# Steps of two head pairs: side jobs between the projections, and their readers moved up on the other engines

## What is computed

```python
h = _layernorm(x) * (1 + ca) + sa
q, k, v = h @ W_q, h @ W_k, h @ W_v
a = sigmoid(h @ W_gate + b_gate)
# per head, over the 256 tokens of a batch
S = a_t[..., None] * S + k_t[..., None] * v_t[..., None, :]
o_t = einsum('bhk,bhkv->bhv', q_t, S)
x = x + ga * (out @ W_o)
h = _layernorm(x) * (1 + cb) + sb
probs = sigmoid(h @ router_w.T + routing_bias); the best TOP_K = 2 of E_ROUTED = 8
x = x + gb * (shared expert(h) + weighted routed experts(h))
```

## Time and profile before

| | us |
|---|---|
| median of 3 runs | 1460.13 |
| lowest, highest | 1457.93, 1462.41 |
| the profiled execution | 1457.31 |
| its span | 1455.2 |
| busy: PE, DVE, POOL, ACT | 1251.1 (86%), 1018.9 (70%), 949.2 (65%), 710.3 (49%) |

### The profile page before, as it was taken

One profiled execution on the slowest core, in us unless ns is written; L12 is line 12 of the kernel. 1 busy time (PEld: TensorE's weight loads), 2 busy tenths in 40 slices (PEclk: granted clock), 3 DMA queues, 4 the chain that ended last, 5 costly groups with the idle time before them and its releaser, 6 DMA issues. The chain is left out here.

```text
span 1455.2 us, 35430 instructions
## 1 busy us (share of the span) xinstructions
PE 1251.1 (86%) x10935; PEld 1086.1 (75%) x10935; DVE 1018.9 (70%) x2183; ACT 710.3 (49%) x1637; POOL 949.2 (65%) x1288
## 2 busy tenths in 40 slices
PE   6999888989888888898989798989797989999970
PEld 5888777777777777776878686868686879889860
DVE  6777767666767676677676666667675647788757
ACT  4665554555454555454545454545454444444420
POOL 4356676758585757676767676766667637777755
PEclk9999999999999999999999999999999999999995
DMA  8900102020111202020202020202021136665336
GB/s 241 262 6 25 60 20 80 23 74 32 65 54 42 83 13 96 2 94 2 94 6 91 7 89 7 89 7 89 17 81 66 49 114 197 192 186 177 100 121 227
DMA packets 88445, 119.30 MB, mean 82 GB/s; under 512 B 9652, under 2 KB 52327, under 8 KB 88384
## 3 DMA queue, kind: packets, MB, share of 16 engines
q1 hardware_dynamic: 79296, 101.47, 22.1%
q0 software_dynamic: 9088, 17.07, 3.4%
HBM read 50.29 MB, written 61.79 MB: 77 GB/s over the span
## 5 line engine op out<-in xcount | busy, mean ns | idle before, releaser
L1188 DVE TENSOR_TENSOR pairs<-qk_banks,pairs 128x512 f32<-128x512 f32 x256 | 164.9, 686 | 131.4 <-PE qk_banks L1536 131.3
L595 POOL TENSOR_SCALAR pairs<-pairs 128x512 f32<-128x512 f32 x128 | 91.8, 717 | 197.7 <-ACT pairs L752 197.4
L1637 PE MATMUL vo_bank<-A,shared 128*64 128x256 f32 (+1 forms) x2048 | 202.6, 342 | 15.4 <-POOL A L510 14.6
L1176 DVE TENSOR_TENSOR_SCAN pairs<-pairs,shared 128x515 f32<-128x515 f32 x128 | 161.7, 1264 | 73.3 <-POOL pairs L593 67.7
L1181 DVE TENSOR_TENSOR_SCAN pairs<-pairs,shared 128x515 f32<-128x515 f32 x128 | 170.4, 1331 | 48.6 <-POOL pairs L595 48.6
L710 POOL DMA_INDIRECT y_dram<-pairs,y_row x156 | 158.0, 1013 | 68.4 <-issue 44.2
L1622 PE MATMUL score_banks<-pairs 64*128 64x128 f32 x2048 | 192.6, 286 | 3.2 <-ACT kx L779 3.2
L1637 PEld LDWEIGHTS vo_bank<-A,shared 128*64 128x64 f32 x2048 | 132.3, 141 | 72.7 <-issue 23.7
L1622 PEld LDWEIGHTS score_banks<-pairs 64*128 64x128 f32 x2048 | 146.6, 188 | 25.6 <-issue 25.6
L1577 PE MATMUL vo_bank<-big,h_hi 128*128 128x512 f32 x128 | 63.4, 495 | 117.9 <-DVE next_row L1160 66.5
L758 ACT ACTIVATE shared<-vo_bank 128x512 f32<-128x512 f32 x128 | 76.4, 597 | 168.9 <-PE vo_bank L1579 168.9
(11 more groups left out here) (252 smaller groups left out, 3241.2 us busy)
## 6 DMA issues: line engine op xcount, KB each, us to landing
rows_dram<-pad_row SPq DMA_DIRECT2D x17, 2112.0 KB, 8.0
ga_all<-rows_dram SPq DMA_DIRECT2D x39, 264.0 KB, 2.8
pairs<-y_dram SPq DMA_DIRECT2D x16, 512.0 KB, 5.0
pairs<-in_L_ffn_gate_w_dram SPq DMA_DIRECT2D x39, 128.0 KB
pairs<-in_L_ffn_up_w_dram SPq DMA_DIRECT2D x39, 128.0 KB
ga_all<-in_L_ffn_down_w_dram SPq DMA_DIRECT2D x39, 128.0 KB, 2.6
mod_rows<-mod_rows_dram SPq DMA_DIRECT2D x32, 128.0 KB, 3.2
h_all<-h_tile SPq DMA_DIRECT2D x16, 256.0 KB, 2.3
```

The lines of the kernel that those rows point to most:

```text
L1176: v.tensor_tensor_scan(G[:, 0:WIDE - 1], gi_t[:, 0:WIDE - 1], cap[:, 0:WIDE - 1], 1.0, ALU.mult, ALU.min)
L1188: v.tensor_tensor(out[:, :, :].rearrange("p u (c t) -> p u c t", c=CHUNKS), QKS[:, :, off:off + T].rearrange("p u (c t) -> p u c t", c=CHU ...
L1637: last = t.matmul(VO[h * DK:(h + 1) * DK, u * T + k * P:(u + 1) * T], v_sb[:, k, vcols], blocks.rearrange("p c t -> p (c t)"), start=(k == ...
```

## The change

Nothing is added to or taken from the computation. In `round_of_steps` of four engines calls change places, and one semaphore (s_xn2) is raised for each half of `normalise2` and no longer once for both, with its counts adapted on SP and POOL. The core of the diff:

```diff
@@ POOL, h_rows
-                alone(s_xn2, k)
+                alone(s_xn2, k * 2 - 1 + u)
@@ POOL, round_of_steps
-                    if s == 5 and one:
+                    if s == 6 and one:
                         h_rows((i - 1) * 2 + 1, i - 1, 1, i)
                     if s >= 5 and two:
-                        scatter_rows(i - 1, s_fill, (i - 1) * 16, ((0,), (1, 2, 3), (4, 5))[s - 5])
+                        scatter_rows(i - 1, s_fill, (i - 1) * 16, ((0, 1), (2, 3), (4, 5))[s - 5])
                     mask_second_head(d)
...
-                    if s == 4 and one:
+                    if s == 5 and one:
                         h_rows((i - 1) * 2, i - 1, 0, i)
@@ ACT, round_of_steps
                     second_head(d)
+                    if s == 4 and two:
+                        write_first_expert(i - 1)
...
-                    if ahead:
-                        exponents(d + 2, p)
-                        tanh_of(d + 2, p, 0)
-                        copy_v(d + 3, 1 if e < 2 else 0, e % 2)
                     if not (last and s == 2 * DUOS - 1):
                         carry_keys(d + 1)
                     if ahead:
+                        exponents(d + 2, p)
+                    if ahead:
+                        copy_v(d + 3, 1 if e < 2 else 0, e % 2)
+                    if ahead:
+                        tanh_of(d + 2, p, 0)
                         tanh_of(d + 2, p, 1)
-                    if s == 4 and two:
-                        write_first_expert(i - 1)
@@ DVE, round_of_steps
                     first_head(d)
+                    if s == 3 and two:
+                        choose(i - 1)
+                    if s == 5 and one:
+                        for u in range(2):
+                            normalise2((i - 1) * 2 + u, u, i)
+                    if e == 0 and more:
+                        normalise(b * CHUNKS + CHUNKS, s_rs, b + 2, s_xn)
                     if not (last and s == 2 * DUOS - 1):
                         products(d + 1)
                     if s == 0 and two:
                         logits(i - 1)
-                    if e == 0 and more:
-                        normalise(b * CHUNKS + CHUNKS, s_rs, b + 2, s_xn)
                     if e == 1 and more:
                         split_h((1 - half) * T, b + 2)
+                    if s == 4 and two:
+                        places(i - 1)
                     if s == 3 and two:
-                        choose(i - 1)
                         weigh(i - 2, i - 1)
...
-                    if s == 4 and two:
-                        places(i - 1)
-                    if s == 4 and one:
-                        for u in range(2):
-                            normalise2((i - 1) * 2 + u, u, i)
...
-                    if e == 3 and not last:
+                    if e == (3 if isinstance(b, int) and b == 0 else 2) and not last:
@@ PE, round_of_steps
                     scores(d)
-                    if ahead:
-                        pe.wait_ge(s_th, d + 2)
-                        if e == 2:
-                            pe.wait_ge(s_hl, b + 2)
-                        project_z((e + 2) % DUOS, half if e < 2 else 1 - half)
                     if not (last and s == 2 * DUOS - 1):
                         project_qk((e + 1) % DUOS, half if e < 3 else 1 - half)
...
                     if s == 0 and two:
                         router(i - 1)
+                    if e == 1 and not (last and half == 1):
+                        xn_transposed(VO, s_xn, b + 2, s_T)
+                    if s == 4 and two:
+                        ranks(i - 1)
+                    if s >= 6 and one:
+                        h_transposed(i, (s - 6) * 2)
+                    if ahead:
+                        pe.wait_ge(s_th, d + 2)
+                        if e == 2:
+                            pe.wait_ge(s_hl, b + 2)
+                        project_z((e + 2) % DUOS, half if e < 2 else 1 - half)
+                    if s == 0 and two:
                         pe.wait_ge(s_lg, i - 1)
```

8 lines of the change are left out of this document (2 added, 6 removed).

## The result

| | median of the runs | from the fastest to the slowest | profiled execution (its span) |
|---|---|---|---|
| before | 1459.45 us | 1457.93 to 1462.41 | 1457.3 (1455.2) |
| after | 1445.34 us | 1443.30 to 1446.16 | 1444.98 (1442.9) |

The ratio is 0.990, 95% interval 0.988 to 0.992: faster by 14 us. Predicted were 1388 us, 1364 to 1422. The sign was right, the size far off and the time outside the range.

What follows compares the result with a forecast made beforehand. PE was taken to bound plain steps (6.90 us), with waits for the places elsewhere. Rounds of 64.7 for 70.06 us gave 69 us in 13 rounds, 69.5 with first and last rounds: 1457.3 to 1388 us, range 1364 to 1422.

Steps and rivals of the forecast that it cites:

- Plain step, 7.42: Steps without extra jobs: attend waits for ACT's late copy of the values, 7.42 us, 0.52 longer than before.
- the copy is not late: Rival on ACT's copy of the values: its chain is shorter than its parts, 1326 us; 8% chance.
- Steps 0, 1, 4: Steps forecast at 8.12, 7.42 and 8.38 us; step 4, 14.71 before, loses the long wait for the places.
- Step 3, 8.74: choose on DVE now precedes the products, so PE stands still about 1.8 us and the step takes 8.74.
- Step 6, 9.3: POOL's h_rows and scatters delay the mask that attend needs; 9.3 us taken, between 8.7 and 9.7.
- the upper of the two cases: Step 6 at 9.7 us: POOL's mask ends up to 1.0 later because GpSimd and VectorE exclude each other.
- Step 5, 7.94: normalise2's four DVE instructions, 1.12 us, stand ahead of the products, adding 0.52 to 7.42.
- Step 7, 7.42: Taken as long as a plain step, 7.42 us; the readers on ACT finish in time.
- the clock falls once per round: Rival: PE's clock drops behind step 3's 1.8 us gap, 14 times at 2.5 us, +35, 1423 us; 8% chance.
- The clock falls again and again: Rival: gaps in every step drop PE's clock three times per round, 45 falls, +114, 1502 us; 5% chance.
- Last round, 1.5 us less: The attention's last round lacks some jobs and its last steps, so its gain was set 1.5 us lower.
- Behind the attention, nothing: What comes after the attention was forecast to stay as it was.

Runs made afterwards that it cites:

- e10: The changed kernel with POOL's update_x moved from ahead of the mask to behind mask and growth in steps 3 and 7; 1447 us.
- e3: The changed kernel with POOL's side jobs of steps 5 to 7 and 0 moved behind mask and growth of the same step; 1406 us.
- e14: The changed kernel with choose in step 2, moments in step 1, and only step 6's POOL side jobs behind mask and growth; 1415 us.
- e6: The changed kernel with choose in step 2, moments in step 1, and POOL's side jobs of steps 5 to 7 and 0 behind mask and growth; 1381 us.
- e13: e6 with the old order (gates first, on PE and ACT) only in rounds 0 and 1, in steps without side jobs; 1369 us.
- e12: e6 with the copy of the values ahead of the two exponents on ACT; 1429 us.

## Why the prediction was right or wrong

Two steps of the prediction failed. It let the clock stay at 1.00 behind the gaps that it had itself forecast, a term of nothing that came to 21 us; and it gave each job the duration, and first_head the place in the step, that they had in the kernel before, so that steps 3, 5, 6 and 7 came out too short. What the runs show in their place: a fall in each of the rounds 2 to 14 at 1.6 us each, and jobs that last longer beside one of the other engine, with no slack left to hide it (step 3 9.37 us without the clock for 8.74, step 6 9.69 for 9.3). Term by term:

**Plain step, 7.42: right**, 7.50 measured; attend waits 0.52 us for L758 as forecast. That *the copy is not late* was ruled out.

**Steps 0, 1, 4: right** within 0.1 (8.04, 7.51, 8.41). The places are no longer late. The term for step 4 was the largest of the sum, and it held.

**Step 3, 8.74: wrong term.** Without the clock it took 9.37. The prediction let first_head end at 1.28, where it had ended in the kernel before, and gave choose 1.84 us. But the second scan of step 2 takes 1.69 us beside update_x, and first_head starts 0.67 us behind the first projection (310.32) and ends at 1.72; choose takes 2.1 us:

```profile
309.38 1.69 DVE L1181 TENSOR_TENSOR_SCAN pairs<-pairs,shared 128x515 f32<-128x515 f32 x1 [0.50 <-POOL pairs L595]
310.99 0.71 DVE L1196 COPY_PREDICATED A<-causal,score_banks 128x512 f32<-128x512 int32 x1
311.61 0.43 DVE L1198 COPY_PREDICATED A<-causal,score_banks 128x256 f32<-128x256 int32 x1
311.93 0.43 DVE L1124 TENSOR_SCALAR lg<-lg_e 128x32 f32<-128x32 f32 x1
...
313.96 0.15 DVE L1134 TENSOR_TENSOR tsum<-top 128x4 f32<-128x4 f32 x1
314.03 1.28 DVE L1188 TENSOR_TENSOR pairs<-qk_banks,pairs 128x512 f32<-128x512 f32 x2
```

PE's gap was 2.4 us, not 1.8. The same scan was as long in the kernel before:

```profile
589.10 1.70 DVE L1181 TENSOR_TENSOR_SCAN pairs<-pairs,shared 128x515 f32<-128x515 f32 x1 [0.57 <-POOL pairs L595]
590.71 0.72 DVE L1196 COPY_PREDICATED A<-causal,score_banks 128x512 f32<-128x512 int32 x1
```

There it ended 0.32 us behind the first projection (590.80 for 590.48) and first_head lost next to nothing. In the new order the gates come behind queries and keys, so the scans end 0.44 us later against ACT's L785 (plain steps of both kernels, medians), and the 0.46 us by which this scan is longer now delay first_head; this shift is what the prediction missed when it took first_head's place over from the old order. The rest is choose's first instruction, L1124: 0.43 us beside POOL's mask (311.57 to 312.33), where the row of before (0.17) had none beside it. e10 shows that update_x beside choose is no cheaper than beside the scan, so the step's length is a sum on DVE and not one unlucky pair.

**Step 6, 9.3: mis-sized**, 9.69 without the clock, the upper of the two cases (9.7). The mask waited behind h_rows and two scatters (its end 6.6 us behind the step's first projection, as in that case), as described; e3 shows it to be the cause. That the total fits the upper case is in part luck: in round 4 L595 ended 1.0 us ahead of the step's first projection where 1.5 were forecast, the first h_rows took 2.5 us where this case has 2.75, and the two scatters took 0.2 less than priced. The row that makes h_rows longer than its 1.75, 0.74 us long in the second h_rows:

```profile
336.56 1.48 POOL L571 TENSOR_TENSOR new_rows<-new_rows,mod_rows 128x256 f32<-128x256 f32 x1
```

In e14 one sees what the step's own sum could not: the jobs of steps 5 to 7 are one queue.

**Step 5, 7.94: mis-sized by 0.45.** The four instructions of normalise2 took 1.65 us where 1.12 were priced. The first scatter stands beside DVE's scan (1.77 us for 1.0), the second and the mask behind it then beside normalise2. Round 4, DVE, then POOL:

```profile
329.40 1.65 DVE L1109 TENSOR_SCALAR new_rows<-xs,mv,rstd 128x128 f32 x4
```

```profile
327.03 1.77 POOL L584 DMA_INDIRECT rows_dram<-token_rows,dest  x1 [0.46 <-issue]
329.10 0.97 POOL L584 DMA_INDIRECT rows_dram<-token_rows,dest  x1 [0.30 <-issue]
330.08 0.88 POOL L510 TENSOR_SCALAR_AFFINE_SELECT A<-A 128x256 f32<-128x256 f32 x2
```

In e3, with the mask first, they take 1.33 and the step 8.08.

**Step 7, 7.42: 7.73.** In e10, where update_x no longer stands ahead of this step's mask, it took 7.50; so update_x is most of it, which the sum had at nothing.

**The clock: the wrong choice.** The rival *the clock falls once per round* had 8% and is what happened, in all rounds from 2 on. Its price, 2.5 us, was too high: 1.6 us. 13 x 1.6 = 21 us of the 57. The reason given against it, that 1.92 us of idle time went by at 1.00, was true but for a shorter gap than those that came, 2.3 to 2.4. Steps 3 and 6 came out 0.6 and 0.4 us longer than forecast before any fall; this cost its own size, and then the clock. *The clock falls again and again* did not happen: after has 13 falls in 13 rounds. (Its 114 us for 45 falls should read 112.5; nothing hangs on it.) By the rule of the Trainium skill ("TensorE: Matmul & The Clock Gate", "A second HAM failure mode: psum-queue depth-cycling") frequent small pauses should make the clock swing. The runs go both ways: e6 and e13 have waits of up to 1.2 us in most steps and no fall in rounds 1 to 14; e12, with waits of 1.14 us in step 7 and 1.0 in step 0, had a fall right behind the latter in seven rounds.

**Last round, 1.5 us less: wrong sign**, 3.9 more. The clock fell twice in it, in steps 3 and 6, and its jobs of steps 5 and 6 are all there:

```profile
1092.00:1095.10 3.10, 0.10 (x2) 0.13 (x4) 0.00 (x0) 0.00 (x0) 2.79 (x6) 0.87 0.13 44
```

In its step 6 PE stands still for 3 us while only POOL works. In e3 and e6 the last round takes 55.9 and 54.2 us.

**Behind the attention, nothing: 4.4 us more**, from the start of its last step. This part took between 338 and 347 us in the kernels here, which have nearly the same instructions in it. Why is not settled. The time up to the attention's first step differed in the same way, by up to 2 us; it was 1.6 us longer in after.

The sums: falls of the clock 21; step 3 another 8, step 6 5, step 5 6, step 7 4 and plain steps 2 (each times 13); last round 5; rounds 0 and 1 3; behind the attention 4; together 58 for the 57 found. The 1.6 us ahead of the first step are not in it; against them stand 1.5 us by which the forecast had rounded its own gain down (69 us for 13 rounds, where 70.16 less 64.74 make 70.5).

## What to carry to other kernels

Before a job is put ahead of a critical instruction, look for a stretch where its engine waits between two links of the loop and put the job there: choose cost 1.9 us (9.37 for 7.50) and a slow clock ahead of the products of step 3, and nothing behind those of step 2. What a queue does has to be summed over all steps that share it, not step by step. Take the place of an instruction over from the old order only if nothing ahead of it moves. Price a gap of PE with what the clock takes behind it, and when a sum leaves a gap near a length that no row has shown at full clock, give the slow case a chance to match.
